# One-core vision layer with a state scan: from state 7 on, every second term made by VectorE in PSUM, the other states' decays in SBUF, scans in one piece

## The chip, the core and the metric

The kernel runs on one core of a Trainium2 chip. Its time is device microseconds from start to end of one execution. The kernel before took 352.08 us, the median of three runs (351.4 to 352.4). One further execution was recorded by the profiler: 354.25 us in all, of which the instructions span 351.9 us. All times below are microseconds unless marked ns.

In the rows, POOL is GpSimd, DVE is VectorE, ACT is ScalarE, PE is TensorE's matmul, PEld its weight load and SP the queue that issues the transfers.

## The reference, cut to what matters

Four images of 1024 tokens with 64 features go through three blocks: token mixing by retention, a selective state scan, and a two-layer feed-forward with routed experts, with a layer norm behind the second and the third. The scan is what the change touches. Per image, with 128 inner channels and 16 states:

```python
x_conv = silu(x_main @ W_conv + b_conv)
B_proj, C_proj = split(x_conv @ W_bc + b_bc)          # 16 states each
dt = softplus(x_conv @ W_dt + b_dt)
def scan_step(h, inputs):                             # over the 1024 tokens
    A_bar = exp(dt_t[..., None] * A)                  # decay
    B_bar = dt_t[..., None] * B_t[:, None, :]
    h_new = A_bar * h + B_bar * x_t[..., None]        # decay * h + term
    y_t = (h_new * C_t[:, None, :]).sum(axis=-1)
```

The kernel takes u = dt * x once per image. For each state s it needs the decay exp(dt * A[:, s]), the term u * B[s], the scan h, and the product hc = h * C[s]; the 16 products are then summed.

## The kernel before

Channels lie on the 128 partitions and tokens on the free dimension, so one state of one image is a job on 128x1024 float32. A `Job` has an image, a state, a first token, a number of halves (of 512 tokens) and `at`, its place counted in halves. Images 0 to 2 have 16 jobs of two halves each. Image 3 is in `SPLIT`: it has 32 jobs of one half, and the change leaves their work as it is.

Each job passes over four engines:

- ScalarE makes the decay (`decay_exp`). It goes either to `slot`, one pair of PSUM banks (the profile calls it `decay`), or to `decay_own` in SBUF.
- The term is made in one of two ways. For a job in `GPSIMD_JOBS`, GpSimd multiplies u by the row of B into the SBUF ring `ub` (`drive` on GpSimd), and the decay is in `slot`. For a job in `VECTOR_JOBS`, ScalarE copies u into `slot` (`fill_slot`), VectorE multiplies it there by the row of B (`drive` on VectorE, the rows `decay<-decay,b_row`), and the decay is in `decay_own`.
- VectorE scans (`scan_job`): h = factor * h + term. In either way one of the two inputs lies in PSUM and the other in SBUF.
- GpSimd makes hc = h * C (`weigh`), and TensorE adds hc up in PSUM (`states_out`).

In images 0 to 2 before, the vector jobs are states 0, 4, 8, 10 and 14. GpSimd has 11 terms and 16 products per image.

There is only one `slot`, so each job's fill waits for the scan of the job before. From state 7 on (`halved`) the scan and the fill go by halves of 512 tokens: ScalarE fills one bank while VectorE scans the other, and the second half's scan starts from the last column of the first.

The order on every engine is written out by hand in steps: phase p is image p's scan, and step n is its state n; k numbers the steps. In step k VectorE scans job k. GpSimd does `weigh` for job k-1 and then `drive` for job k+1, so the order of its queue is: product of k-1, term of k+1, product of k, term of k+2, and so on, with no term where the job is a vector job. ScalarE fills the slot for job k+1 near the start of step k and makes the `decay_own` of job k+2 at its end. VectorE's queue in the same steps also carries the head of the next image (`weight_scores` in steps 0 to 7, `prelu` in 8, `step_sizes` in 12, `inputs` in 13, which makes the next u) and the tail of the image before (`last_part`). The b and c rows come by transfers from SP three and two steps ahead.

In this document "product k" is the POOL instruction hc of state k, "term k" is the POOL instruction ub of state k, and "the late part" of an image is what runs from its state 7 to state 0 of the next image.

Of the kernel before, what the change touches and what calls it, by code (L numbers as in the profile page):

```python
# [46 lines left out]
for _b in range(IMAGES):  # L47
    for _first in (0, HALF) if _b in SPLIT else (0,):
        for _s in range(STATES):
# [7 lines left out]
               if job.state in ((0, 4, 8, 10, 14) if job.image not in SPLIT else range(0, STATES, 2))]  # L57
# [70 lines left out]
def vit_layer(nc, xT, gammaT, packed, routed_w, route, out):  # L128
    with ExitStack() as ctx:
        def sb(name, shape, dt=F32):  # L130
            return ctx.enter_context(nc.sbuf_tensor(name, shape, dt))
# [39 lines left out]
        ub = sb("ub", [P, 3 * T])  # L171
        decay_own = sb("decay_own", [P, T])
# [133 lines left out]
        def end_of(q):  # L306
            return JOBS[q].at + JOBS[q].halves
# [31 lines left out]
        def halved(q):  # L339

            return JOBS[q].halves == 2 and JOBS[q].state >= TILES - 1
# [5 lines left out]
        def ring(at, halves):  # L347

            return slice(at % 6 * HALF, (at % 6 + halves) * HALF)

# [547 lines left out]
        def _(act):  # L898
# [20 lines left out]
            def own_decay(q):  # L919

                made, halves = vector_made(q), JOBS[q].halves
                if made >= 2:

                    act.wait_ge(scan_done, end_of(job_with(vector_made, VECTOR_JOBS, made + halves - 3)))
                decay_exp(q, decay_own[:, two_banks(made, halves)], tokens(q))

            def fill_slot(q):

                job = JOBS[q]
                if on_vector(q) and job.state == 0 and job.first == 0:  # L930
                    act.wait_ge(u_ready, job.image + 1)
                if q == 0:
                    act.wait_ge(next_read, 3)
                in_halves = job.halves == 2 and q > 0 and halved(q - 1)
                for at, halves in ((job.at, 1), (job.at + 1, 1)) if in_halves else ((job.at, job.halves),):
                    if at + halves > 2:

                        act.wait_ge(scan_done, at + halves - 2)
                    first = job.first + (at - job.at) * HALF
                    columns = slice(first, first + halves * HALF)  # L940
                    if on_vector(q):
                        nc.scalar.activation(slot[:, two_banks(at, halves)], u[:, job.image % 2, columns], ACT.Copy)\  # L942
                            .then_inc(u_copied, halves)
                    else:
                        decay_exp(q, slot[:, two_banks(at, halves)], columns)
# [164 lines left out]
            for p in PHASES:  # L1110
                for n in range(STEPS):
# [3 lines left out]
                    for i, (start, end) in enumerate(parts(p, n)):  # L1115
                        for q in begun(start + 2, end + 2):
                            fill_slot(q)
# [23 lines left out]
                        for q in range(len(JOBS)):  # L1141
                            if own_limit(start) <= JOBS[q].at < own_limit(end) and on_vector(q):
                                own_decay(q)
# [19 lines left out]
        def _(pool):  # L1163
# [17 lines left out]
            def drive(q):  # L1181
# [6 lines left out]
                if made + job.halves > 6:  # L1188

                    pool.wait_ge(scan_done, end_of(job_with(gpsimd_made, GPSIMD_JOBS, made + job.halves - 7)))  # L1190
                nc.gpsimd.tensor_tensor(ub[:, ring(made, job.halves)], u[:, job.image % 2, tokens(q)],  # L1191
# [25 lines left out]
        def _(dve):  # L1217
# [88 lines left out]
            def scan_job(q):  # L1306

                job = JOBS[q]
                for at, halves in ((job.at, 1), (job.at + 1, 1)) if halved(q) else ((job.at, job.halves),):
                    done = at + halves - job.at  # L1310
                    here = two_banks(at, halves)
                    if on_vector(q):
                        drive(q, here, ring(at, halves), vector_made(q) + done)
                        factor, term = decay_own[:, two_banks(vector_made(q) + at - job.at, halves)], slot[:, here]
                    else:
                        dve.wait_ge(ub_ready, gpsimd_made(q) + job.halves)
                        factor, term = slot[:, here], ub[:, ring(gpsimd_made(q) + at - job.at, halves)]
                    dve.wait_ge(decay_ready, at + halves)
                    if at + halves > 6:
                        dve.wait_ge(hc_ready, at + halves - 6)  # L1320
                        old = JOBS[JOB_OF[at + halves - 7]]
                        if old.halves == 1 and old.first == 0:
                            dve.wait_ge(carry_saved, old.state + 1)
                    initial = 0.0
                    if at > job.at:
                        dve.wait_ge(scan_done, at)
                        initial = h[:, ring(at - 1, 1).stop - 1:ring(at - 1, 1).stop]
                    elif job.first:
                        dve.wait_ge(carry_saved, job.state + 1)
                        initial = carry[:, job.state:job.state + 1]  # L1330
                    nc.vector.tensor_tensor_scan(h[:, ring(at, halves)], factor, term, initial, ALU.mult, ALU.add)\  # L1331
                        .then_inc(scan_done, halves)
# [223 lines left out]
```

## Time and profile before

| | |
|---|---|
| median of three runs | 352.08 us |
| profiled execution, whole / its span | 354.25 / 351.9 us |
| POOL busy | 259.5 us (74%), 136 instructions |
| DVE busy | 262.4 us (75%), 287 instructions |
| ACT busy | 191.0 us (54%), 298 instructions |
| PE busy | 280.4 us (80%), 1426 instructions |
| mean granted TensorE clock | 0.902 |

Busy shares are averages over unlike stages. The scans of images 0 to 2 fill the span from about 45 to 255 us, and there the busy digits of DVE and POOL are 8 or 9 nearly throughout. Matmuls are pipelined, so PE's share is not a measure of its peak. A stretch is best read from where a given product starts to where a later one starts, since GpSimd does them in a fixed order.

### The profile page before, as it was taken

The numbers are of one execution on the slowest core, as the hardware profiler recorded it, in microseconds if no ns is written. First come the engines' busy times: TensorE is split into PE (matmuls) and PEld (weight loads), VectorE is DVE, ScalarE is ACT, GpSimd is POOL, SyncE is SP. The second block draws the span as 40 slices with busy tenths as digits, with TensorE's granted clock in tenths as the row PEclk, the third lists the DMA queues.
The fourth block names the chain that finished last, engine by engine and source line by source line (L and its number), as shares of the span: only waits on it lengthen the run. The fifth ranks groups of instructions, "written<-read, shape, count | busy, mean of one in ns | idle before, by whom it ended". The sixth has DMA issues, their size and how long they took to land.

```text
span 351.9 us, 4676 instructions
## 1 busy us (share of the span) xinstructions
PE 280.4 (80%) x1426; PEld 160.4 (46%) x1426; DVE 262.4 (75%) x287; ACT 191.0 (54%) x298; POOL 259.5 (74%) x136
## 2 busy tenths in 40 slices
PE   8998838784965889998895999977647846887996
PEld 5423402332453343465632434756434535636664
DVE  2466669989778989987989899879988766249420
ACT  2105823337895243689674337893785843357532
POOL 1027067998999999999999799899978889349300
PEclk9999959998789899999999899987976995588999
DMA  7960596766699997776999877678999999536200
GB/s 234 417 258 0 160 313 225 236 249 257 226 306 304 278 394 270 240 277 193 325 307 374 284 239 235 244 233 278 321 304 313 296 309 340 163 122 177 45 2 15
DMA packets 47128, 85.88 MB, mean 244 GB/s; under 512 B 7936, under 2 KB 24832, under 8 KB 46848
## 3 DMA queue, kind: packets, MB, share of 16 engines
q1 hardware_dynamic: 46704, 84.43, 72.8%
q10 hardware_dynamic: 400, 1.17, 1.1%
q8 instruction: 11, 0.18, 0.2%
q14 instruction: 13, 0.11, 0.1%
HBM read 75.62 MB, written 1.57 MB: 219 GB/s over the span
## 4 chain that ended last, share of the span: by engine, by line
PE 24%; DVE 13%; ACT 9%; DMA 6%; issue 4%; POOL 3%; SPq 2%; DVEq 0%; POOLq 0%; ACTq 0%
DVE h L1331 9%; PE acc_y L661 5%; PE tail L720 4%; DMA c_row<-bc_dram 4%; POOL ub L1191 2%; PE acc_r L614 2%; DMA b_row<-bc_dram 2%; PE work L603 2%; DVE decay L1303 2%; ACT decay L915 1%; PE work L752 1%; POOL hc L1202 1%; PE decay L537 1%; ACT decay_own L915 1%; ACT decay L942 1%
## 5 line engine op out<-in xcount | busy, mean ns | idle before, releaser
L1202 POOL TENSOR_TENSOR hc<-h,c_row 128x1024 f32<-128x1024 f32 (+1 forms) x79 | 154.3, 1961 | 30.0 <-DVE h L1331 24.4
L1191 POOL TENSOR_TENSOR ub<-u,b_row 128x1024 f32<-128x1024 f32 (+1 forms) x49 | 98.1, 2003 | 17.2 <-DVE u L1377 11.6
L661 PEld LDWEIGHTS acc_y<-pack,hc 128*128 128x128 f32 x512 | 63.8, 154 | 48.7 <-issue 34.7
L661 PE MATMUL acc_y<-pack,hc 128*128 128x128 f32 x512 | 78.2, 298 | 9.4 <-ACT y_t L1025 4.9
L915 ACT ACTIVATE decay<-delta,neg_a 128x512 f32<-128x512 f32 (+1 forms) x64 | 51.3, 812 | 62.7 <-DVE h L1331 62.1
L1331 DVE TENSOR_TENSOR_SCAN h<-decay,ub 128x512 f32<-128x512 f32 (+1 forms) x41 | 66.0, 1609 | 12.4 <-POOL ub L1191 6.4
L603 PE MATMUL work<-q,kT 64*128 64x512 f32 x112 | 33.7, 679 | 18.4 <-DVE mixed L1357 14.1
L942 ACT ACTIVATE decay<-u 128x512 f32<-128x512 f32 (+1 forms) x42 | 26.5, 640 | 30.4 <-DVE h L1331 30.2
L1303 DVE TENSOR_TENSOR decay<-decay,b_row 128x512 f32<-128x512 f32 (+1 forms) x40 | 30.8, 769 | 14.4 <-DMA b_row<-bc_dram 8.6
L1357 DVE TENSOR_TENSOR mixed<-gam,work 128x512 f32<-128x512 f32 x56 | 35.5, 676 | 7.9 <-PE work L603 7.1
L614 PE MATMUL acc_r<-mixed,v_sb 128*64 128x512 f32 x128 | 36.9, 657 | 1.1 <-DVE mixed L1357 1.0
L1331 DVE TENSOR_TENSOR_SCAN h<-decay_own,decay 128x512 f32<-128x512 f32 (+1 forms) x23 | 34.5, 1498 | 1.1
L915 ACT ACTIVATE decay_own<-delta,neg_a 128x512 f32<-128x512 f32 (+1 forms) x31 | 28.5, 918 | 1.5 <-DVE delta L1370 1.4
L720 PEld LDWEIGHTS tail<-f,group_w 128*128 128x128 f32 x192 | 27.6, 221 | 0.4
L720 PE MATMUL tail<-f,group_w 128*128 128x64 f32 x192 | 26.8, 301 | 0.0
L1331 DVE TENSOR_TENSOR_SCAN h<-decay,h,ub 128x512 f32<-128x512 f32 x18 | 23.1, 1283 | 2.5
L603 PEld LDWEIGHTS work<-q,kT 64*128 64x128 f32 x112 | 8.9, 193 | 34.2 <-DVE mixed L1357 23.9
L1176 POOL TENSOR_TENSOR expert_w<-expert_w 128x2048 f32<-128x2048 f32 x2 | 9.0, 4520 | 15.3 <-DMA expert_w<-routed_w 15.3
L614 PEld LDWEIGHTS acc_r<-mixed,v_sb 128*64 128x64 f32 x128 | 6.6, 141 | 26.6 <-issue 18.2
L715 PE MATMUL tail<-onehot,bias_w 96*128 96x512 bf16 x12 | 5.1, 426 | 14.2 <-ACT f L1055 7.1
L1331 DVE TENSOR_TENSOR_SCAN h<-decay_own,h,decay 128x512 f32<-128x512 f32 x9 | 11.5, 1280 | 0.3
L981 ACT ACTIVATE hT<-acc_r,pack 128x512 f32<-128x512 f32 x4 | 2.7, 675 | 15.8 <-PE acc_r L614 15.8
(206 smaller groups left out, 347.0 us busy)
## 6 DMA issues: line engine op xcount, KB each, us to landing
b_row<-bc_dram SPq DMA_DIRECT2D x64, 512.0 KB, 5.3
c_row<-bc_dram SPq DMA_DIRECT2D x64, 512.0 KB, 5.9
group_w<-expert_w SPq DMA_DIRECT2D x48, 128.0 KB, 5.0
gam<-gammaT SPq DMA_DIRECT2D x8, 512.0 KB, 10.6
expert_w<-routed_w SPq DMA_DIRECT2D x1, 2048.0 KB, 18.4
gam<-expert_w SPq DMA_DIRECT2D x16, 128.0 KB, 4.7
x_in<-xT SPq DMA_DIRECT2D x4, 256.0 KB, 9.0
pack<-packed ACTq DMA_DIRECT2D x1, 788.0 KB, 6.7
```

The costliest lines, as they stand in the source:

```text
L603: nc.tensor.matmul(pair[:, i * HALF:(i + 1) * HALF], kT[D * i:D * i + D, j * P:(j + 1) * P], q2[D * i:D * i + D, :], start=True, stop=True ...
L614: mm = nc.tensor.matmul(acc_r[D * i:D * i + D, :], v_sb[:, j, :], mixed[:, j % 2, i * HALF:(i + 1) * HALF], start=(j == 0), stop=(j == TIL ...
L661: mm = nc.tensor.matmul(acc_y[:, to:to + P], hc[:, at:at + P], ident, start=(job.state == 0 and c % 4 == 0), stop=(job.state == STATES - 1 ...
L720: mm = nc.tensor.matmul(bank[:, (g % 8) * GROUP:(g % 8 + 1) * GROUP], group_w[:, g, layer, :], f[:, g * GROUP:(g + 1) * GROUP], start=Fals ...
L915: op = nc.scalar.activation(target, delta[:, job.image % 2, columns], ACT.Exp, scale=neg_a[:, job.state:job.state + 1])
L942: nc.scalar.activation(slot[:, two_banks(at, halves)], u[:, job.image % 2, columns], ACT.Copy)\
L1176: nc.gpsimd.tensor_tensor(w, w, expert_w[:, layer, EXPERTS, :].unsqueeze(1) .broadcast_to([P, EXPERTS, HID]), ALU.add).then_inc(s_cw, 1)
L1191: nc.gpsimd.tensor_tensor(ub[:, ring(made, job.halves)], u[:, job.image % 2, tokens(q)], b_row[:, ring(job.at, job.halves)], ALU.mult).the ...
L1202: nc.gpsimd.tensor_tensor(hc[:, here], h[:, here], c_row[:, here], ALU.mult).then_inc(hc_ready, job.halves)
L1303: nc.vector.tensor_tensor(slot[:, here], slot[:, here], b_row[:, columns], ALU.mult).then_inc(ub_own, halves)
L1331: nc.vector.tensor_tensor_scan(h[:, ring(at, halves)], factor, term, initial, ALU.mult, ALU.add)\
L1357: nc.vector.tensor_tensor(mixed[:, j % 2, at], gam[:, j, at], pair[:, at], ALU.mult).then_inc(read, 1)
```

## The change

In images 0 to 2:

- State 12 becomes a vector job too, so that from state 8 on all even states are, and GpSimd has 10 terms per image instead of 11.
- `KEPT_JOBS` are the jobs whose decay is kept in SBUF: all vector jobs and, new, the GpSimd jobs 7, 9, 11, 13 and 15. Those five have their decay in `decay_own` and their term in `ub`, and do not use `slot` at all. `SLOT_JOBS` are the jobs that do use it.
- `decay_own` has room for two whole jobs instead of one (a ring of four halves, `two_rows`), and `ub` for two instead of three.
- The slot's fill waits for the last job that used the same bank (`slot_left`), not for the job before.
- `halved` goes: from state 7 on scans, multiplies, fills and copies cover all 1024 tokens in one instruction.

```diff
 VECTOR_JOBS = [q for q, job in enumerate(JOBS)
-               if job.state in ((0, 4, 8, 10, 14) if job.image not in SPLIT else range(0, STATES, 2))]
+               if job.state in ((0, 4, 8, 10, 12, 14) if job.image not in SPLIT else range(0, STATES, 2))]
+KEPT_JOBS = [q for q, job in enumerate(JOBS)
+             if q in VECTOR_JOBS or job.image not in SPLIT and job.state in (7, 9, 11, 13, 15)]
+SLOT_JOBS = [q for q in range(len(JOBS)) if q in VECTOR_JOBS or q not in KEPT_JOBS]
...
-        ub = sb("ub", [P, 3 * T])
-        decay_own = sb("decay_own", [P, T])
+        ub = sb("ub", [P, 2 * T])
+        decay_own = sb("decay_own", [P, 2 * T])
...
+        def kept_made(q):
+
+            return sum(JOBS[s].halves for s in KEPT_JOBS if s < q)
+
+        def slot_left(q):
+
+            used = [s for s in SLOT_JOBS if s < q and (JOBS[q].halves == 2 or JOBS[s].halves == 2
+                                                       or JOBS[s].at % 2 == JOBS[q].at % 2)]
+            return end_of(used[-1]) if used else 0
...
+        def two_rows(made, halves):
+
+            return slice(made % 4 * HALF, (made % 4 + halves) * HALF)
...
             def own_decay(q):
 
-                made, halves = vector_made(q), JOBS[q].halves
-                if made >= 2:
-
-                    act.wait_ge(scan_done, end_of(job_with(vector_made, VECTOR_JOBS, made + halves - 3)))
-                decay_exp(q, decay_own[:, two_banks(made, halves)], tokens(q))
+                made, halves = kept_made(q), JOBS[q].halves
+                if made + halves > 4:
+
+                    act.wait_ge(scan_done, end_of(job_with(kept_made, KEPT_JOBS, made + halves - 5)))
+                decay_exp(q, decay_own[:, two_rows(made, halves)], tokens(q))
...
-                in_halves = job.halves == 2 and q > 0 and halved(q - 1)
-                for at, halves in ((job.at, 1), (job.at + 1, 1)) if in_halves else ((job.at, job.halves),):
-                    if at + halves > 2:
-
-                        act.wait_ge(scan_done, at + halves - 2)
...
+                if slot_left(q):
+                    act.wait_ge(scan_done, slot_left(q))
+                if on_vector(q):
+                    nc.scalar.activation(slot[:, two_banks(job.at, job.halves)], u[:, job.image % 2, tokens(q)], ACT.Copy)\
+                        .then_inc(u_copied, job.halves)
+                else:
+                    decay_exp(q, slot[:, two_banks(job.at, job.halves)], tokens(q))
...
             def scan_job(q):
 
                 job = JOBS[q]
...
+                here, end = two_banks(job.at, job.halves), end_of(q)
+                if on_vector(q):
+                    drive(q, here, ring(job.at, job.halves), vector_made(q) + job.halves)
+                    term = slot[:, here]
+                else:
+                    dve.wait_ge(ub_ready, gpsimd_made(q) + job.halves)
+                    term = ub[:, two_rows(gpsimd_made(q), job.halves)]
+                dve.wait_ge(decay_ready, end)
+                factor = decay_own[:, two_rows(kept_made(q), job.halves)] if q in KEPT_JOBS else slot[:, here]
...
+                nc.vector.tensor_tensor_scan(h[:, ring(job.at, job.halves)], factor, term, initial, ALU.mult, ALU.add)\
+                    .then_inc(scan_done, job.halves)
```

On VectorE's queue in image 0, from state 7 to state 10 (a scan is listed there as SCALAR_TENSOR_TENSOR with h on the left), before:

```order
L1331 SCALAR_TENSOR_TENSOR h<-decay,ub 128x512
L1331 SCALAR_TENSOR_TENSOR h<-decay,h,ub 128x512
L1303 TENSOR_TENSOR decay<-decay,b_row 128x512
L1331 SCALAR_TENSOR_TENSOR h<-decay_own,decay 128x512
L1303 TENSOR_TENSOR decay<-decay,b_row 128x512
L1331 SCALAR_TENSOR_TENSOR h<-decay_own,h,decay 128x512
L1362 SCALAR_TENSOR_TENSOR hT<-acc_r,neg_ba,hT 128x512
L1331 SCALAR_TENSOR_TENSOR h<-decay,ub 128x512
L1331 SCALAR_TENSOR_TENSOR h<-decay,h,ub 128x512
```

and after:

```order
L1336 SCALAR_TENSOR_TENSOR h<-decay_own,ub 128x1024
L1312 TENSOR_TENSOR decay<-decay,b_row 128x1024
L1336 SCALAR_TENSOR_TENSOR h<-decay_own,decay 128x1024
L1367 SCALAR_TENSOR_TENSOR hT<-acc_r,neg_ba,hT 128x512
L1336 SCALAR_TENSOR_TENSOR h<-decay_own,ub 128x1024
L1312 TENSOR_TENSOR decay<-decay,b_row 128x1024
L1336 SCALAR_TENSOR_TENSOR h<-decay_own,decay 128x1024
```

The scans of states 7 and 9 read both inputs from SBUF (`decay_own` and `ub`), a form that VectorE's queue before does not hold; those of 8 and 10 keep one input in PSUM.

On GpSimd's queue in image 0, from product 9 to product 13 (term k is ub, product k is hc), before:

```order
L1202 TENSOR_TENSOR hc<-h,c_row 128x1024
L1191 TENSOR_TENSOR ub<-u,b_row 128x1024
L1202 TENSOR_TENSOR hc<-h,c_row 128x1024
L1191 TENSOR_TENSOR ub<-u,b_row 128x1024
L1202 TENSOR_TENSOR hc<-h,c_row 128x1024
L1191 TENSOR_TENSOR ub<-u,b_row 128x1024
L1202 TENSOR_TENSOR hc<-h,c_row 128x1024 x2
```

and after:

```order
L1211 TENSOR_TENSOR hc<-h,c_row 128x1024
L1200 TENSOR_TENSOR ub<-u,b_row 128x1024
L1211 TENSOR_TENSOR hc<-h,c_row 128x1024 x2
L1200 TENSOR_TENSOR ub<-u,b_row 128x1024
L1211 TENSOR_TENSOR hc<-h,c_row 128x1024 x2
```

Before, this reads product 9, term 11, product 10, term 12, product 11, term 13, products 12 and 13. After, term 12 is gone: product 9, term 11, products 10 and 11, term 13, products 12 and 13.

## Rows read from the trace of the kernel before

**Rows 1.** The page's busy times: us, share of the span, instructions.

```profile
PE 280.4 (80%) x1426; PEld 160.4 (46%) x1426; DVE 262.4 (75%) x287; ACT 191.0 (54%) x298; POOL 259.5 (74%) x136
```

**Rows 2.** Busy time by stretch: from product 7 to the next image's product 0 (three rows), then from product 0 to product 7 (images 1, 2).

```profile
core 0: us, PE busy (x) PEld busy (x) DVE busy (x) ACT busy (x) POOL busy (x), PEclk, DMA share, GB/s
80.60:118.22 37.62, 25.84 (x121) 14.64 (x120) 31.33 (x31) 26.51 (x40) 35.73 (x15) 0.83 0.82 276
148.16:186.42 38.26, 33.00 (x206) 21.07 (x204) 33.79 (x35) 29.37 (x45) 35.78 (x16) 1.00 0.84 274
217.62:255.28 37.66, 30.12 (x182) 21.66 (x182) 33.08 (x35) 28.51 (x45) 35.84 (x17) 0.91 0.82 267
118.22:148.16 29.94, 27.59 (x135) 12.32 (x133) 27.50 (x27) 14.47 (x17) 28.00 (x12) 0.99 0.90 299
186.42:217.62 31.20, 27.80 (x131) 11.90 (x132) 28.14 (x27) 14.85 (x17) 27.93 (x12) 0.95 0.83 283
```

**Rows 3.** POOL in order of time, image 1's products 6, 7: start, us, instruction, [idle before].

```profile
145.32 2.36 POOL L1202 TENSOR_TENSOR hc<-h,c_row 128x1024 f32<-128x1024 f32 x1
148.16 2.35 POOL L1202 TENSOR_TENSOR hc<-h,c_row 128x1024 f32<-128x1024 f32 x1 [0.49 <-DVE h L1331]
150.47 2.36 POOL L1191 TENSOR_TENSOR ub<-u,b_row 128x1024 f32<-128x1024 f32 x1
152.78 2.36 POOL L1202 TENSOR_TENSOR hc<-h,c_row 128x1024 f32<-128x1024 f32 x1
```

**Rows 4.** Who waited for whom, 148.16 to 186.42: total us, times, longest.

```profile
POOL hc L1202 <- DVE h L1331: 3.0, 5, 0.9
...
DVE h L1331 <- POOL ub L1191: 1.2, 2, 1.0
...
DVE decay L1303 <- ACT decay L942: 0.8, 1, 0.8
```

**Rows 5.** Groups of the whole span by form: busy us, mean ns, idle before.

```profile
L1331 DVE TENSOR_TENSOR_SCAN h<-decay_own,decay 128x1024 f32<-128x1024 f32 x6 | 13.7, 2286 | 0.5
...
L1331 DVE TENSOR_TENSOR_SCAN h<-decay,h,ub 128x512 f32<-128x512 f32 x18 | 23.1, 1283 | 2.5
L1331 DVE TENSOR_TENSOR_SCAN h<-decay_own,decay 128x512 f32<-128x512 f32 x17 | 20.7, 1220 | 0.6
...
L1303 DVE TENSOR_TENSOR decay<-decay,b_row 128x1024 f32<-128x1024 f32 x6 | 7.4, 1229 | 1.2 <-issue 1.1
```

**Rows 6.** Groups by form on ACT: exponentials and copies, half and whole.

```profile
L915 ACT ACTIVATE decay<-delta,neg_a 128x512 f32<-128x512 f32 x46 | 31.2, 691 | 14.9 <-DVE h L1331 14.5
...
L915 ACT ACTIVATE decay_own<-delta,neg_a 128x1024 f32<-128x1024 f32 x15 | 17.1, 1137 | 1.4 <-DVE delta L1370 1.4
...
L942 ACT ACTIVATE decay<-u 128x512 f32<-128x512 f32 x38 | 22.4, 599 | 22.4 <-DVE h L1331 22.4
...
L942 ACT ACTIVATE decay<-u 128x1024 f32<-128x1024 f32 x4 | 4.1, 1028 | 8.0 <-DVE h L1331 7.8 <-DVE u L1377 0.2
```

**Rows 7.** DVE where u is made in images 0, 1 and 2.

```profile
105.00 1.20 DVE L1377 TENSOR_TENSOR u<-delta,mixed 128x1024 f32<-128x1024 f32 x1
...
172.57 1.20 DVE L1377 TENSOR_TENSOR u<-delta,mixed 128x1024 f32<-128x1024 f32 x1
...
242.49 1.20 DVE L1377 TENSOR_TENSOR u<-delta,mixed 128x1024 f32<-128x1024 f32 x1
```

**Rows 8.** POOL at the same three places, product 13.

```profile
105.22 3.20 POOL L1202 TENSOR_TENSOR hc<-h,c_row 128x1024 f32<-128x1024 f32 x1 [0.49 <-DVE h L1331]
...
172.79 3.20 POOL L1202 TENSOR_TENSOR hc<-h,c_row 128x1024 f32<-128x1024 f32 x1 [0.50 <-DVE h L1331]
...
242.71 3.19 POOL L1202 TENSOR_TENSOR hc<-h,c_row 128x1024 f32<-128x1024 f32 x1 [0.50 <-DVE h L1331]
```

**Rows 9.** ACT's copy of u for state 10, and DVE's last scan of state 13, image 1.

```profile
156.05 1.12 ACT L942 ACTIVATE decay<-u 128x512 f32<-128x512 f32 x2
...
171.38 1.28 DVE L1331 TENSOR_TENSOR_SCAN h<-decay,h,ub 128x512 f32<-128x512 f32 x1
```

**Rows 10.** DVE in image 1: the scan of state 8's second half, then prelu.

```profile
150.50 1.28 DVE L1331 TENSOR_TENSOR_SCAN h<-decay_own,h,decay 128x512 f32<-128x512 f32 x1
151.69 0.73 DVE L1362 SCALAR_TENSOR_TENSOR hT<-acc_r,neg_ba,hT 128x512 f32<-128x512 f32 x1
```

More of the change, by code:

```diff
@@ L337, in job_with @@
             return [q for q in jobs if made(q) <= piece < made(q) + JOBS[q].halves][0]
-        def halved(q):
-            return JOBS[q].halves == 2 and JOBS[q].state >= TILES - 1
+        def kept_made(q):
[4 more added lines that the diff above has]
+            return end_of(used[-1]) if used else 0
         def ub_made(q):
@@ L933, in fill_slot @@
                     act.wait_ge(next_read, 3)
-                in_halves = job.halves == 2 and q > 0 and halved(q - 1)
-                for at, halves in ((job.at, 1), (job.at + 1, 1)) if in_halves else ((job.at, job.halves),):
-                    if at + halves > 2:
-                        act.wait_ge(scan_done, at + halves - 2)
[L939 to L945, printed above, removed]
+                if slot_left(q):
[5 more added lines that the diff above has]
+                    decay_exp(q, slot[:, two_banks(job.at, job.halves)], tokens(q))
             def save_carry(q):
@@ L1141, in _ @@
                         for q in range(len(JOBS)):
-                            if own_limit(start) <= JOBS[q].at < own_limit(end) and on_vector(q):
+                            if own_limit(start) <= JOBS[q].at < own_limit(end) and q in KEPT_JOBS:
                                 own_decay(q)
@@ L1187, in drive @@
                 pool.wait_ge(b_loaded[k % 3], 16 * (k // 3 + 1))
-                if made + job.halves > 6:
-                    pool.wait_ge(scan_done, end_of(job_with(gpsimd_made, GPSIMD_JOBS, made + job.halves - 7)))
-                nc.gpsimd.tensor_tensor(ub[:, ring(made, job.halves)], u[:, job.image % 2, tokens(q)],
+                if made + job.halves > 4:
+                    pool.wait_ge(scan_done, end_of(job_with(gpsimd_made, GPSIMD_JOBS, made + job.halves - 5)))
+                nc.gpsimd.tensor_tensor(ub[:, two_rows(made, job.halves)], u[:, job.image % 2, tokens(q)],
                                         b_row[:, ring(job.at, job.halves)], ALU.mult).then_inc(ub_ready, job.halves)
@@ L1308, in scan_job @@
                 job = JOBS[q]
[L1309 to L1332, printed above, removed]
@@ new lines, in scan_job @@
+                if end > 6:
+                    dve.wait_ge(hc_ready, end - 6)
+                    old = JOBS[JOB_OF[end - 7]]
+                    if old.halves == 1 and old.first == 0:
+                        dve.wait_ge(carry_saved, old.state + 1)
+                initial = 0.0
+                if job.first:
+                    dve.wait_ge(carry_saved, job.state + 1)
+                    initial = carry[:, job.state:job.state + 1]
+                nc.vector.tensor_tensor_scan(h[:, ring(job.at, job.halves)], factor, term, initial, ALU.mult, ALU.add)\
+                    .then_inc(scan_done, job.halves)
```

3 lines of the change are left out of this document (2 added, 1 removed).

## The prediction

> **What bounds the kernel now.** I read the busy times first, then the stretches of the scans, then GpSimd's queue in order of time, then the waits. The page shows DVE and POOL nearly equal, 262.4 and 259.5 us of 351.9 [rows 1]: neither can be called the bound from that. The stretches tell more. In the late part of each image (product 7 to the next image's product 0, 37.62, 38.26 and 37.66 us, mean 37.85) POOL is busy 35.7 to 35.8 us and DVE 31.3 to 33.8 [rows 2]. In the early part DVE and POOL are both near 28 of 30 to 31 us. So in the late part, the only one that the change rewrites, GpSimd is the fullest engine: 9 products and 6 terms of 2.36 us, one behind the other at a spacing of 2.31 (150.47 to 152.78) [rows 3]. What is left of the 38.26 us is 3.0 us in which a product waited for its scan, in 5 pieces [rows 4]. DVE waits for terms 1.2 us and for the copy of u 0.8 us there, so the single slot costs DVE little; it is POOL's queue that sets the pace.
>
> **What the change takes off.** By form, the two halves of a scan take 1.22 + 1.28 = 2.50 us and one whole scan 2.29 [rows 5]: 0.21 less for each of 27 scans (9 late states, 3 images), 5.7 us of DVE. The multiply in PSUM takes 1.23 us whole [rows 5]; the three new ones (state 12) cost DVE 3.7 us. DVE so gains about 2 us over three images, on an engine that has 4 to 6 us of slack per late part [rows 2]: worth nothing by itself. On POOL three terms go, 3 x 2.31 = 6.9 us, and these are on the path. ACT pays 1.14 us for a kept decay in place of 2 x 0.69, and 1.03 for a copy in place of 2 x 0.60 [rows 6]; state 12 adds it a copy, 0.8 us net. ACT is busy 29.4 of 38.3 us [rows 2], so either sign is hidden, except for one place, below. The exponential for job k+2 now waits for scan k and stands at the end of ScalarE's step k; behind it in its queue are the copy for job k+2 and the tail's pieces of step k+1. Before, the second half of each fill waited for the same scan k and stood earlier in the step, so nothing on ACT gets later by it. The ub ring of two costs nothing: GpSimd's term k+1 is issued behind product k-1, whose scan is at or behind the last reader of the buffer it reuses.
>
> **What it adds: scans with both inputs in SBUF.** 15 scans (states 7, 9, 11, 13, 15 of three images) now read `decay_own` and `ub`. No scan before does. The nearest rows are the three u = delta * x, the DVE instructions with two SBUF inputs that run beside GpSimd. At 105.00, 172.57 and 242.49 u takes its usual 1.20 us [rows 7], and POOL's product 13, which starts 0.22 us later, takes 3.20, 3.20 and 3.19 [rows 8] instead of 2.36 [rows 3]. That is 0.84 us more, of the 0.98 that it lies beside u. Products beside other DVE work (scans and multiplies with an operand in PSUM) all keep 2.35 to 2.38. So GpSimd stands nearly still while VectorE reads two operands from SBUF.
>
> The bounds for one such scan: nothing (2.29 us on DVE, POOL undisturbed; I see no reason for a gain), up to 2.29 us of POOL at a standstill plus a whole POOL instruction, 2.36, for which DVE waits first. I take a standstill of the whole scan, by the u rows, and work out from the queue's order what of DVE's wait counts.
>
> The Trainium skill, "SBUF — State Buffer", section "Who interferes with whom", says that a VectorE instruction with two SBUF inputs contends with a GpSimd instruction that reads SBUF, and that the shared port pair is held by one of them for the whole instruction, whoever was first. The trace agrees for the case in which VectorE was first (0.84 us); GpSimd first is not shown by any row before. By this rule the sum would be the one below; its opposite is a rival.
>
> **The walk of one pair of states**, t = 0 where term 9 is done. GpSimd goes on with product 8 at once (scan 8 is done by then), so scan 9 and product 8 want SBUF together. In whichever order, one after the other: 2.31 + 2.29 us. Product 9 waits for scan 9, hands over in 0.13 us (scan 13 ends at 171.38 + 1.28 = 172.66 [rows 9], product 13 starts at 172.79 [rows 8]), and is followed by term 11. VectorE's multiply and scan of state 10 (1.23 + 2.29) fall beside those two undisturbed, since one of their operands is in PSUM. The pair costs POOL three instructions and a standstill, 3 x 2.31 + 2.29 + 0.17 (0.13 and 0.04 for the way to DVE) = 9.4 us. DVE needs 5.8 us for the pair, up to 2.3 of waiting, and at most 1.95 of other work in the steps 11 and 12: 10.1 us, but scan 13 then meets product 12 still running, so POOL's count holds.
>
> **The sum.** Product 7 to the next product 0: 14 POOL instructions x 2.31 = 32.3; four standstills (scans 9, 11, 13, 15) x 2.46 = 9.8; and the 0.84 beside u as before. Together 43.0 against 37.85: +5.1 us. The standstill of scan 7 lies before product 7: product 6 to product 7 takes 2.31 + 2.46 = 4.8 us instead of 2.84 (145.32 to 148.16) [rows 3]: +1.9. Per image +7.0 to +7.2, in three images +21 to +22. The other check: 5 x 2.46 = 12.3 added, one term (2.3) and the idle of 2.8 absorbed, 7.2. The early parts (29.94 and 31.20 us) have about 2 to 3 us of idle on POOL [rows 2], but the product order couples them to scans of their own, so I give nothing back. On the profiled execution, 354.25 + 21.7 = 376; on the median, which is 2.2 lower, 352.1 + 21.7 = 373.8. I forecast 374.
>
> **The one place on ACT.** Scan 8 ends at 150.50 + 1.28 = 151.8 [rows 10], and the copy of u for state 10 starts at 156.05, behind the table load and the convolution [rows 9]. With 1.03 for a whole copy, the multiply of state 10 can start 5.3 us after scan 8's end. In the walk scan 9 ends about 5.9 us after scan 8's end, so this is just hidden. If scan 9 isn't held up, that cover is gone, which enters the first rival.
>
> **Rivals.**
>
> *A. No contention (faster).* The scan doesn't keep GpSimd from SBUF, because it is not a plain multiply. For it: the scan takes 2.29 us for 1024 columns where a multiply takes 1.23 [rows 5], so it asks for data half as often. Against it: the u rows. Then the pair costs POOL 3 x 2.31 + 0.14 = 7.1 us. Late part: 32.3 + 0.84 + 0.14 x 4, plus about 1.4 us where DVE is late by step sizes and two tail pieces before scan 13, and 0.7 from the copy of state 10: 35.8 to 36.5, which is 1.4 to 2.0 less than 37.85. Three images: -4 to -6, 347 us. This decides if the standstill per scan is below about 0.4 us.
>
> *B. Each element read costs GpSimd a cycle, no lock.* For 1024 elements POOL loses what it lost beside u, 0.84 to 0.98 us, once per scan, and goes on in between; DVE never waits. For it: the u rows fit just as well, since a multiply asks for data all the time. Against A's 35.8 to 36.5: four times 0.9 less some 0.9 that falls in DVE's late pieces, +2.7, and +0.9 before product 7. Late part about 38.9, product 6 to 7 unchanged to +0.5: +1.1 to +1.5 per image, +4: 356 us.
>
> *C. More than the walk.* Waits on both sides don't overlap: each of the 15 scans also delays a later one by the 2.36 us of DVE's wait. That bounds it above: 374 + 15 x 2.36 = 409. The walk excludes most of it, since DVE has 3.6 us of slack per pair (9.4 against 5.8).
>
> That the change doesn't do what it says isn't open: the queues of the changed kernel show the form `h<-decay_own,ub`.
>
> **Chances and range.** The standstill (likeliest) 0.68, own range 366 to 384: the low end if the early parts give back 2 to 3 us per image, the high end if DVE's wait counts four or five times. A 0.17, B 0.11, C (above 384) 0.04. The range of 8 in 10: 347 to 383, which leaves out C and half of A. A difference of 0.3% is 1.1 us, about what a measurement of this kernel can tell from no change. Faster by more than that: A and a sliver of B, 0.18. Within: 0.04. Slower: 0.78.
>
> **What would show it.** The scans `h<-decay_own,ub` read longer than 2.29 us, up to 4.6 (GpSimd first), or POOL's products beside them read up to 4.6 us instead of 2.36 (DVE first). The late part goes from 37.85 to about 43 us, product 6 to 7 from 2.84 to 4.8; POOL instructions per late part go from 15 to 14; the early parts stay at 30 to 31, and image 3 is unchanged. DVE's scans with a PSUM operand stay at 2.29. The forecast is wrong if the new scans read 2.29 and POOL keeps 2.36 beside them (A), or if POOL's products read about 3.2 (B).

## The result, and the profile after

The changed kernel takes 368.57 us, the median of four runs (368.1 to 370.3; a fifth took 366.8), beside 352.24 us for the kernel before (four runs). The ratio is 1.046, with a 95% interval of 1.041 to 1.051: slower by 16 us. The profiled execution took 370.3 us, its span 368.2. The forecast was 374 us and a standstill of GpSimd beside the new scans. A few executions, of the kernel before and of one other, ran some per cent slower as a whole; every ratio, and the times of the last run of experiment 7, leave them out.

The page's busy line of the changed kernel:

```profile
PE 296.0 (80%) x1426; PEld 173.6 (47%) x1426; DVE 287.4 (78%) x254; ACT 189.6 (51%) x275; POOL 254.5 (69%) x133
```

DVE has 33 instructions fewer than in [rows 1] and is busy 25.0 us longer. The groups by form say where that is. The first of these DVE groups is the new form (columns as in [rows 5]):

```profile
L1336 DVE TENSOR_TENSOR_SCAN h<-decay_own,ub 128x1024 f32<-128x1024 f32 x15 | 63.0, 4201 | 8.5 <-POOL ub L1200 6.0 <-issue 2.1 <-ACT decay_own L928 0.3
L1336 DVE TENSOR_TENSOR_SCAN h<-decay_own,decay 128x1024 f32<-128x1024 f32 x18 | 41.2, 2286 | 1.6
```

The scan with one input in PSUM reads 2.29 us as before. The same scan with both inputs in SBUF reads 4.20 in the mean. GpSimd in order of time, image 0, from product 6 on:

```profile
77.65 2.36 POOL L1211 TENSOR_TENSOR hc<-h,c_row 128x1024 f32<-128x1024 f32 x1
82.29 2.35 POOL L1211 TENSOR_TENSOR hc<-h,c_row 128x1024 f32<-128x1024 f32 x1 [2.28 <-DVE h L1336]
84.60 2.36 POOL L1200 TENSOR_TENSOR ub<-u,b_row 128x1024 f32<-128x1024 f32 x1
86.91 2.35 POOL L1211 TENSOR_TENSOR hc<-h,c_row 128x1024 f32<-128x1024 f32 x1
91.54 2.36 POOL L1211 TENSOR_TENSOR hc<-h,c_row 128x1024 f32<-128x1024 f32 x1 [2.28 <-DVE h L1336]
```

and VectorE beside the first of them:

```profile
77.79 4.37 DVE L1336 TENSOR_TENSOR_SCAN h<-decay_own,ub 128x1024 f32<-128x1024 f32 x1 [0.97 <-issue]
82.08 1.20 DVE L1312 TENSOR_TENSOR decay<-decay,b_row 128x1024 f32<-128x1024 f32 x1
```

Product 6 starts at 77.65 and ends at 80.01. Scan 7 starts 0.14 us after it, at 77.79, and ends at 82.16: it makes its 2.15 us of progress once product 6 is over. Only then can product 7 go. This repeats at every second state, so a pair of states takes 9.25 us from product to product (82.29 to 91.54), and 9.25 to 9.28 wherever the prediction's walk applies, against its 9.4. The stretches that answer to [rows 2] (late part of images 0, 1, 2, then image 1's early part with product 6 to 7):

```profile
82.29:124.87 42.58, 27.04 (x112) 14.74 (x112) 38.56 (x21) 24.49 (x30) 33.42 (x14) 0.73 0.79 252
155.95:198.65 42.70, 35.47 (x196) 23.59 (x196) 40.05 (x25) 26.80 (x34) 33.50 (x14) 0.88 0.80 252
231.31:273.66 42.35, 31.12 (x170) 23.46 (x171) 39.47 (x26) 26.50 (x36) 35.51 (x16) 0.82 0.79 257
124.87:155.95 31.08, 29.34 (x147) 13.26 (x145) 29.11 (x26) 16.54 (x20) 27.98 (x13) 0.99 0.81 278
```

| stretch | before | after | difference | forecast |
|---|---|---|---|---|
| three late parts | 113.54 | 127.63 | +14.1 | +15.3 |
| product 6 to 7, three times | 8.55 | 13.96 | +5.4 | +5.7 |
| product 0 to 6, three times | 83.77 | 82.77 | -1.0 | 0 |
| image 3, from its first product to the end | 96.62 | 94.54 | -2.1 | 0 |

The prediction's terms per image, 5.1 and 1.9, make 21.0 in this table; it went on with 21.7, from its other check. With the first product 0.12 us earlier, this is the whole 16.3 us between the spans.

The last late part shows the other order, in which a GpSimd instruction finds VectorE's scan before it. At the seam to image 3 GpSimd has a half-size term behind product 14, while scan 15 (started at 264.71, 4.38 us) is waiting:

```profile
264.59 2.35 POOL L1211 TENSOR_TENSOR hc<-h,c_row 128x1024 f32<-128x1024 f32 x1
266.90 3.25 POOL L1200 TENSOR_TENSOR ub<-u,b_row 128x512 f32<-128x512 f32 x1
```

That term takes 1.27 us elsewhere. Here scan 15 gets its turn when product 14 ends, and the term loses 1.98 us to it. This is far more than the 0.84 to 0.98 that rival B allowed for the reads of one scan.

### The profile page after: what moved, and what is told of

Same layout as the page of the kernel before. It is cut to its first block and busy times, and to the rows that moved or that the text cites. A ratio compares the mean times of both kernels' runs of the same rounds, so it can differ in the third digit from the quotient of the medians.

```text
span 368.2 us, 4607 instructions
## 1 busy us (share of the span) xinstructions
PE 296.0 (80%) x1426; PEld 173.6 (47%) x1426; DVE 287.4 (78%) x254; ACT 189.6 (51%) x275; POOL 254.5 (69%) x133
## 5 line engine op out<-in xcount | busy, mean ns | idle before, releaser
L674 PE MATMUL acc_y<-pack,hc 128*128 128x128 f32 x512 | 83.3, 311 | 15.3 <-POOL hc L1211 11.6
L1336 DVE TENSOR_TENSOR_SCAN h<-decay_own,ub 128x1024 f32<-128x1024 f32 x15 | 63.0, 4201 | 8.5 <-POOL ub L1200 6.0
L928 ACT ACTIVATE decay_own<-delta,neg_a 128x1024 f32<-128x1024 f32 (+1 forms) x49 | 49.1, 1004 | 22.6 <-DVE h L1336 18.0
L928 ACT ACTIVATE decay<-delta,neg_a 128x512 f32<-128x512 f32 (+1 forms) x31 | 27.8, 897 | 51.2 <-DVE h L1336 51.0
L1336 DVE TENSOR_TENSOR_SCAN h<-decay_own,decay 128x1024 f32<-128x1024 f32 (+1 forms) x26 | 50.9, 1958 | 1.9
L1336 DVE TENSOR_TENSOR_SCAN h<-decay,ub 128x1024 f32<-128x1024 f32 (+1 forms) x23 | 44.0, 1911 | 3.4 <-ACT decay L928 2.7
L1312 DVE TENSOR_TENSOR decay<-decay,b_row 128x1024 f32<-128x1024 f32 (+1 forms) x34 | 32.8, 966 | 8.0 <-DMA b_row<-bc_dram 4.6
L950 ACT ACTIVATE decay<-u 128x1024 f32<-128x1024 f32 (+1 forms) x34 | 28.0, 825 | 20.3 <-DVE h L1336 20.1
L733 PEld LDWEIGHTS tail<-f,group_w 128*128 128x128 f32 x192 | 35.9, 278 | 1.6 <-issue 0.7
L733 PE MATMUL tail<-f,group_w 128*128 128x64 f32 x192 | 34.6, 359 | 0.0
L1336 DVE TENSOR_TENSOR_SCAN h<-decay_own,carry,decay 128x512 f32<-128x512 f32 x8 | 10.2, 1280 | 0.3
```

The source lines that it names most:

```text
L674: mm = nc.tensor.matmul(acc_y[:, to:to + P], hc[:, at:at + P], ident, start=(job.state == 0 and c % 4 == 0), stop=(job.state == STATES - 1 ...
L733: mm = nc.tensor.matmul(bank[:, (g % 8) * GROUP:(g % 8 + 1) * GROUP], group_w[:, g, layer, :], f[:, g * GROUP:(g + 1) * GROUP], start=Fals ...
L928: op = nc.scalar.activation(target, delta[:, job.image % 2, columns], ACT.Exp, scale=neg_a[:, job.state:job.state + 1])
L950: nc.scalar.activation(slot[:, two_banks(job.at, job.halves)], u[:, job.image % 2, tokens(q)], ACT.Copy)\
L1312: nc.vector.tensor_tensor(slot[:, here], slot[:, here], b_row[:, columns], ALU.mult).then_inc(ub_own, halves)
L1336: nc.vector.tensor_tensor_scan(h[:, ring(job.at, job.halves)], factor, term, initial, ALU.mult, ALU.add)\
```

## The experiments

All are changes of one of the two kernels; their times stand beside runs of the kernel before on the same chip (352.1 to 353.6 us in the median), and a ratio is to those.

### 1. The decays go to the slot again

```diff
 KEPT_JOBS = [q for q, job in enumerate(JOBS)
-             if q in VECTOR_JOBS or job.image not in SPLIT and job.state in (7, 9, 11, 13, 15)]
+             if q in VECTOR_JOBS]
```

> The changed kernel, but the decays of states 7, 9, 11, 13 and 15 go into the PSUM slot again (scans in one piece, state 12 by VectorE, two-deep ub stay). Theory (a scan with both inputs in SBUF and a GpSimd instruction cannot run side by side): the late scans read 2.29 us again instead of 4.36, GpSimd's 2.28 us of idle before every second product goes, and what remains is ScalarE's fill in series with a whole scan, about 1.1 us per late state where VectorE has no other work: 350 to 358 us. Rival (the loss comes from the whole scans, from state 12 on VectorE or from the shallower ub): the time stays at 365 to 372 us.

Measured: 365.47 us (363.7 to 368.9), ratio 1.035 (1.029 to 1.041). The trace did what the theory said of the holds: all scans of 1024 tokens read 2.28 to 2.29 us. But the time is far above the expected 350 to 358 and lies in the rival's range, 365 to 372. These are its DVE groups and its three late parts:

```profile
L1336 DVE TENSOR_TENSOR_SCAN h<-decay,ub 128x1024 f32<-128x1024 f32 x30 | 68.7, 2289 | 14.6 <-ACT decay L928 13.3 <-POOL ub L1200 1.3
...
L1312 DVE TENSOR_TENSOR decay<-decay,b_row 128x1024 f32<-128x1024 f32 x18 | 22.1, 1230 | 16.5 <-ACT decay L950 11.2 <-issue 5.2
```

```profile
80.10:121.14 41.04, 29.44 (x124) 17.44 (x124) 31.00 (x21) 26.67 (x33) 33.55 (x14) 0.72 0.80 262
150.31:195.12 44.81, 39.28 (x206) 26.37 (x205) 33.40 (x25) 29.65 (x38) 33.64 (x14) 0.85 0.83 261
225.98:267.33 41.35, 31.54 (x176) 23.30 (x175) 31.23 (x24) 28.44 (x37) 33.72 (x16) 0.83 0.77 253
```

In the whole span these groups wait 24.5 us for ScalarE's fills (13.3 + 11.2). In the three late parts alone VectorE waits 22.3 us for fills, where the kernel before has 6.8. So a loss of 12 us stands without a single hold. It isn't the whole scans' alone: state 12 on VectorE is in it too, and by itself it costs 8 us (experiment 2), so whole scans and the shallower `ub` add about 4. Image 1 is 3.5 us longer than the others and has the granted clock at 0.50 from 172 to 180 (see experiment 4). The changed kernel pays for holds, this one for fills.

### 2. State 12 by VectorE, alone in the kernel before

```diff
-               if job.state in ((0, 4, 8, 10, 14) if job.image not in SPLIT else range(0, STATES, 2))]
+               if job.state in ((0, 4, 8, 10, 12, 14) if job.image not in SPLIT else range(0, STATES, 2))]
```

> The kernel before with one part of the change alone: state 12's term by VectorE in PSUM, all else as before (halves, one slot, ub of three). Theory (GpSimd's queue sets the pace of the late part): one term of 2.31 us less per image, of which VectorE's two multiplies of 0.69 us take back a part: late part 36.0 to 37.3 us instead of 37.85, total 346 to 351 us. Rival (VectorE and GpSimd bound it together): 351 to 355 us, no gain or a small loss.

Measured: 361.28 us (359.7 to 363.9), ratio 1.023 (1.019 to 1.028). Both theories are wrong: it is 8 us slower. GpSimd has one instruction less per late part, and the late parts are longer:

```profile
80.30:119.68 39.38, 28.17 (x122) 17.06 (x121) 32.53 (x33) 27.45 (x41) 33.53 (x14) 0.75 0.85 268
149.34:191.38 42.04, 35.72 (x206) 23.77 (x204) 35.14 (x37) 30.21 (x46) 33.59 (x14) 0.92 0.82 265
222.62:262.11 39.49, 31.60 (x181) 23.38 (x182) 33.91 (x36) 29.29 (x45) 33.65 (x15) 0.83 0.82 262
```

Product 11 to product 12 goes from 4.63 us to 6.01. ScalarE there, in image 1 (start, us, instruction):

```profile
162.75 0.45 ACT L967 ACTIVATE mixed<-acc_r,pack 128x256 f32<-128x256 f32 x1
...
164.81 0.67 ACT L1014 ACTIVATE work<-work,pack 128x512 f32<-128x512 f32 x1
165.38 1.17 ACT L915 ACTIVATE decay_own<-delta,neg_a 128x1024 f32<-128x1024 f32 x1
166.42 1.14 ACT L942 ACTIVATE decay<-u 128x512 f32<-128x512 f32 x2
```

and VectorE:

```profile
164.84 0.67 DVE L1392 TENSOR_SCALAR f<-tail 128x512 f32<-128x512 f32 x1
167.07 0.70 DVE L1303 TENSOR_TENSOR decay<-decay,b_row 128x512 f32<-128x512 f32 x1 [1.56 <-ACT decay L942]
```

At the same place in the kernel before, scan 12 starts with

```profile
165.37 1.22 DVE L1331 TENSOR_TENSOR_SCAN h<-decay,ub 128x512 f32<-128x512 f32 x1 [1.04 <-POOL ub L1191]
```

ScalarE is busy without a gap from the eviction of B and C through the softplus pieces, the exponential and the copy. VectorE's multiply waits 1.56 us for that copy (1.56 in image 2 too, 2.15 in image 0). The two multiplies and this wait come to 2.9 us in VectorE's chain, where before a wait of 1.04 us for GpSimd's term stood: +1.8 us, the difference of the late parts of images 0 and 2. In image 1 the clock comes on top (experiment 4). The chain scan 11, scan 12, scan 13 was as near the bound as GpSimd's queue, and products cannot run ahead of scans.

### 3. A shorter copy

```diff
+                        cut = 64 if job.state == 12 and job.halves == 2 else halves * HALF
```

> State 12 alone on VectorE, and ScalarE copies only 64 of every 512 tokens of u for state 12 (the rest of that state's term is left out, so this measures the wait, not a whole kernel). Theory (ScalarE's queue of softplus pieces, exponential and copy makes VectorE's multiply of state 12 late by 1.6 us, so the cover that the prediction gave ScalarE's work isn't there): VectorE's wait before that multiply falls from 1.56 us to 0.4 to 1.2, and product 11 to product 12 from 6.01 us to 5.0 to 5.6. Rival (VectorE's own work makes it long): product 11 to 12 stays above 5.8.

Measured (one run of 356.66 us, which has no interval): the wait falls only to 1.19 us in images 1 and 2, and product 11 to 12 from 6.01 to 5.63 there. In image 0 the wait hardly falls (2.15 to 2.11), and product 11 to 12 stays at 5.97. That is at or just beyond the weak end of what the theory expected, and below the rival's 5.8 in two images of three. The copy itself is a small part; what stands ahead of it in ScalarE's queue is the larger one, as the rows above suggest. How the rest divides is not settled.

### 4. TensorE's clock in image 1

In experiment 2 the late part of image 1 is 2.6 us longer than the other two. The granted clock stands at 0.50 (the 1.2 GHz level) there. In the 4 us before it fell TensorE was busy 1.7 us, where in the same 4 us of the kernel before it was busy 3.0 and the clock stayed at 1.00:

```profile
168.00:170.00 2.00, 0.57 (x6) 0.33 (x4) 1.97 (x3) 1.97 (x3) 1.75 (x1) 1.00 0.81 311
170.00:172.00 2.00, 1.13 (x2) 0.30 (x2) 2.00 (x3) 1.72 (x4) 0.93 (x1) 1.00 0.71 156
172.00:178.00 6.00, 4.99 (x24) 4.91 (x25) 5.38 (x7) 2.41 (x4) 3.78 (x2) 0.50 1.03 307
```

The edit on top of experiment 2 repeats products with the same result:

```diff
-                    mm = queries(acc_r)
+                    for _ in range(3):
+                        mm = queries(acc_r)
...
-                    mm = keys(use == SIDE_K1, acc_r[:, :])
+                    for _ in range(4 if use == SIDE_K0 else 1):
+                        mm = keys(use == SIDE_K1, acc_r[:, :])
```

> State 12 alone on VectorE (as in the run before), and TensorE does the queries' products of step 11 three times and the first keys' product of step 12 four times over, with the same results, to keep it busy there. Theory (the late part of image 1 is 2.6 us longer than that of images 0 and 2, 42.0 against 39.4, because the granted clock stands at 0.5 from 172 to 178 us): the clock stays at 1.0 there, the late part of image 1 falls to 39.3 to 40.5 us and the time by 1 to 3 us, to 358 to 360. Rival (the clock costs nothing, ScalarE or the transfers make it long): the late part of image 1 keeps 41.5 us or more. The late parts of images 0 and 2 change by less than 1 us in either case.

```profile
150.59:190.52 39.93, 36.99 (x220) 22.84 (x218) 35.06 (x37) 30.12 (x46) 33.58 (x14) 1.00 0.84 259
```

The clock stays at 1.00, and the late part of image 1 falls from 42.04 to 39.93 us, level with the others (39.82 and 39.31). VectorE's one wait for TensorE's `work` in that late part, near its end, falls from 1.92 to 0.48 us. So the slower step brought a slower clock with it, and the clock cost about 2.1 us. The total is 360.40 us (358.8 to 360.5), ratio 1.025 (1.019 to 1.031): against 1.023 (1.019 to 1.028) this doesn't resolve as a gain.

The same edit on the changed kernel:

> The changed kernel with the same repeated products. Theory (its late parts are set by GpSimd's instructions and the scans with two SBUF inputs one after the other, so TensorE's clock is hidden): late part of image 1 from 42.70 to 42.5 to 42.8 us, time within 1.5 us of 368.6, whatever the clock does. Rival (the clock has a part in the loss of the changed kernel): it falls by 2 us or more.

Measured: 371.01 us (370.7 to 371.7), ratio 1.055 (1.049 to 1.061), so 2.4 us slower. Both the time (within 1.5 us was expected) and the late part of image 1 (44.00 us, 42.5 to 42.8 expected) were misses. Nor did the edit hold the clock at 1.00. Here is the low stretch of the changed kernel, then that of this run:

```profile
173.00:181.60 8.60, 6.61 (x27) 5.82 (x28) 8.36 (x8) 3.32 (x4) 6.99 (x3) 0.52 0.79 234
...
174.40:181.20 6.80, 5.78 (x26) 5.67 (x27) 6.56 (x8) 2.36 (x3) 6.29 (x3) 0.50 0.70 244
```

So this run can't tell what the clock costs. Images 0 and 2 keep their late parts (42.57 and 42.33); in image 1, 1.3 us come between product 13 and 14 (6.85 in place of 5.57), where product 14 waits 1.34 us for TensorE: the repeated products got in the way there. The changed kernel's own trace tells more. Its three pairs of states from product 7 to 13 of image 1 take the same time, whatever the clock:

```profile
155.95:165.22 9.27, 8.42 (x58) 6.23 (x58) 9.02 (x6) 6.53 (x8) 6.99 (x3) 1.00 0.61 221
165.22:174.49 9.27, 4.52 (x26) 1.89 (x24) 7.78 (x4) 9.21 (x12) 6.99 (x4) 0.94 0.62 202
174.49:183.76 9.27, 8.77 (x35) 7.37 (x36) 9.03 (x8) 3.26 (x5) 6.99 (x4) 0.51 0.78 241
```

What it costs behind product 13 isn't shown apart; that late part is 0.1 us longer than image 0's.

### 5. What the 4.37 us of a scan are

The products that GpSimd does beside the new scans, cut to 64 tokens:

```diff
+                if job.halves == 2 and job.state in (6, 8, 10, 12, 14):
+                    here = slice(here.start, here.start + 64)
```

> The changed kernel with products 6, 8, 10, 12 and 14 of images 0 to 2 cut to the first 64 of 1024 tokens (their rest is left out, so this measures the scans, not a whole kernel). Theory (the 4.36 us of a scan with both inputs in SBUF are 2.1 us of waiting for the product that GpSimd started just before): these scans read 2.2 to 2.5 us, and GpSimd still idles about 2.3 us before the next product. Rival (the form itself is slow, with two SBUF inputs): they keep 4.2 to 4.4 us.

```profile
L1338 DVE TENSOR_TENSOR_SCAN h<-decay_own,ub x15: 2269/2292/2341, 77.5 to 255.3; 128x1024 f32<-128x1024 f32 x15
```

All 15 (min, median, max in ns) read the 2.29 us of any whole scan. The form is not slow; its time went into waiting for the product. GpSimd still idles 2.28 us and more before the next product. The run took 359.36 us (one run, without an interval), in spite of five products per image being cut to a sixteenth: late parts of 38.3, 43.8 and 39.3 us, as VectorE again waits for ScalarE (2.23 us before the multiply of state 10 in image 0).

The same products in two instructions:

```diff
+                    for i in range(2):
+                        part = slice(here.start + i * HALF, here.start + (i + 1) * HALF)
+                        nc.gpsimd.tensor_tensor(hc[:, part], h[:, part], c_row[:, part], ALU.mult).then_inc(hc_ready, 1)
```

> The changed kernel with products 6, 8, 10, 12 and 14 of images 0 to 2 as two GpSimd instructions of 512 tokens. Theory (SBUF is held for one instruction, and VectorE gets its turn between two of GpSimd's): the scans with both inputs in SBUF read 3.2 to 3.4 us instead of 4.36 (1.1 left of the first half, 2.15 of its own), the second half of the product reads 3.2 to 3.4 instead of 1.27, GpSimd's idle before the next product goes from 2.28 to under 0.3, and the time is within 1.5 us of 368.6, since the two still run one after the other. Rival (VectorE waits until GpSimd's queue has a gap): the scans keep 4.4 us and more. Rival (no hold, each element read costs a cycle): the second half reads at most 1.27 + 1.07 us and the time falls below 364.

```profile
159.21 3.28 DVE L1341 TENSOR_TENSOR_SCAN h<-decay_own,ub 128x1024 f32<-128x1024 f32 x1 [0.90 <-POOL ub L1200]
```

```profile
159.08 4.48 POOL L1214 TENSOR_TENSOR hc<-h,c_row 128x512 f32<-128x512 f32 x2
163.52 2.36 POOL L1216 TENSOR_TENSOR hc<-h,c_row 128x1024 f32<-128x1024 f32 x1
```

The two halves take 4.48 us instead of about 2.5 (two of 1.27) and end one behind the other with the scan between them. The scan reads 3.28 us: the rest of the first half and its own; the second half reads 3.25. So the hold lasts one instruction, and whoever waits comes next. The time, 366.62 us (366.1 to 368.7), ratio 1.038 (1.033 to 1.043), is 2 us below the changed kernel, a little more than the 1.5 expected: product 6 to product 7, which holds one standstill, takes 4.44 instead of 4.65 us.

### 6. One hold more, and one term more

State 12 by GpSimd with its decay in SBUF too:

```diff
-               if job.state in ((0, 4, 8, 10, 12, 14) if job.image not in SPLIT else range(0, STATES, 2))]
+               if job.state in ((0, 4, 8, 10, 14) if job.image not in SPLIT else range(0, STATES, 2))]
...
-             if q in VECTOR_JOBS or job.image not in SPLIT and job.state in (7, 9, 11, 13, 15)]
+             if q in VECTOR_JOBS or job.image not in SPLIT and job.state in (7, 9, 11, 12, 13, 15)]
```

> The changed kernel with state 12 left to GpSimd (its decay in SBUF too, so states 11, 12 and 13 scan with both inputs in SBUF): six such scans per image instead of five, eleven terms instead of ten. Theory (GpSimd's instructions and these scans run one after the other): one more term of 2.31 and one more standstill of 2.28 us per image, +13 to +15 us on 368.6: 381 to 384 us. Rival (the scans of this form cost a fixed loss that other work hides): +0 to +7, up to 376.

Measured: 379.17 us (378.5 to 380.6), ratio 1.073 (1.065 to 1.080). That is 2 us below the expected 381 to 384 and above the rival's 376. The late parts are 46.53, 46.56 and 46.28 us, +3.9 each, where +4.6 was expected. Scans 11 and 12 now hold up a term that stands directly behind a product:

```profile
98.24 4.33 POOL L1200 TENSOR_TENSOR ub<-u,b_row 128x1024 f32<-128x1024 f32 x1
```

Such a term loses 1.98 us, where GpSimd otherwise loses 2.32 from product to product (4.63 less 2.31). One term of 2.31 and one standstill of 1.98 more, and 0.34 less for scan 11's, make 3.95. Image 3 gave back 2.9 us.

State 12 by GpSimd with its decay in the slot, the five other holds kept (the first of the two edits alone):

> The changed kernel without its state-12 part: state 12's term by GpSimd again, its decay in the PSUM slot, the five scans with two SBUF inputs stay. Theory (with these scans, GpSimd's instructions and the scans in one line set the late part): one term of 2.31 us more per image, late part 42.5 to 44.9, +6 to +8 us on 368.6, so 374.5 to 377; the same part that made the kernel before 8 us slower is worth 7 us here. Rival (state 12 on VectorE costs here too, through ScalarE's queue, as it did alone): 360 to 368 us.

```profile
96.01 4.37 DVE L1336 TENSOR_TENSOR_SCAN h<-decay_own,ub 128x1024 f32<-128x1024 f32 x1 [1.40 <-POOL ub L1200]
102.62 2.29 DVE L1336 TENSOR_TENSOR_SCAN h<-decay,ub 128x1024 f32<-128x1024 f32 x1 [2.24 <-POOL ub L1200]
```

```profile
95.87 2.36 POOL L1211 TENSOR_TENSOR hc<-h,c_row 128x1024 f32<-128x1024 f32 x1
98.19 4.34 POOL L1200 TENSOR_TENSOR ub<-u,b_row 128x1024 f32<-128x1024 f32 x1
```

Measured: 372.18 us (371.6 to 374.4), ratio 1.062 (1.052 to 1.071), below the expected 374.5 to 377 and clearly above the rival's 368. The late parts are 44.55, 44.59 and 44.27, +1.9 each: a term of 2.31, less the 0.34 by which scan 11 costs GpSimd less when a term stands behind the product. Product 10 at 95.87 holds up scan 11; scan 11 then holds up term 12 (4.34 us instead of 2.36): the two are strictly in one line. Image 3 gave back 4.4 us against the changed kernel (90.19 and 94.54). The same move of state 12, which costs the kernel before 8 us, saves 3.6 us here.

### 7. Two tries for a faster kernel

Whole scans only where VectorE has other work behind, on top of experiment 2:

```diff
-            return JOBS[q].halves == 2 and JOBS[q].state >= TILES - 1
+            return JOBS[q].halves == 2 and JOBS[q].state >= TILES - 1 and JOBS[q].state not in (8, 12, 13)
```

> The kernel before with state 12's term by VectorE, and with the scans of states 8, 12 and 13 in one piece, where VectorE has other work behind the scan (prelu, step sizes, u) that covers ScalarE's fill of the slot. Theory: VectorE saves 0.21 us per whole scan and 0.13 per whole multiply, about 1 us per image, which counts where VectorE is now the later one: 0 to 3 us below the kernel with state 12 alone, 345 to 350 us. Rival (the fill is not covered): 1 to 3 us above it.

Measured: 364.64 us (362.4 to 367.3), ratio 1.031 (1.026 to 1.036). The theory failed: it is 3.4 us above experiment 2, just past the rival's 3. Late parts of 40.5, 45.9 and 40.4 us. VectorE waits 13.5 us for ScalarE's fills in them, where in experiment 2 it waits 11.9. In image 1 the granted clock is at 0.50 from 172 to 184, so the 45.9 is not the fills' alone.

The loads of the last image's weights two steps later, in the kernel before:

```diff
-                    if p == ALONE and n < TILES:
-                        for g in (2 * n, 2 * n + 1):
+                    if p == ALONE and 2 <= n < TILES + 2:
+                        for g in (2 * n - 4, 2 * n - 3):
```

> The kernel before, with the 16 loads of the last image's expert weights issued in steps 2 to 9 of image 3 instead of 0 to 7. Theory (image 3 is shorter after the change, 94.5 against 96.6 us, because SP's queue had caught up by then and the b rows came in time): moving other transfers off the first steps gives a part of this without the change: the waits for b rows (8.6 us on VectorE, 4.1 on GpSimd in the profile of before) fall and the time goes down by 0.5 to 2 us, to 350.5 to 352. Rival (the rows are late for want of transfer bandwidth, not of turns in SP's queue): within 0.5 us of the kernel before, or slower.

Measured: 350.80 us (348.4 to 353.3), ratio 0.998 (0.993 to 1.002). In the profile image 3 takes 93.9 us instead of 96.62, and VectorE's waits for b rows fall from 8.6 to 4.8 us, but the time does not resolve from that of the kernel before. No kernel of this study is shown to be faster.

## Why the prediction was right, and where it was wrong

- **GpSimd stands still beside a scan with two SBUF inputs: right**, and shown in both orders. The walk of a pair gave 9.4 us; the trace has 9.27. By the Trainium skill ("SBUF — State Buffer", "Who interferes with whom") the pair of ports is held for the whole instruction by whoever was first. The traces agree: 1.98 us lost by a term behind scan 15, 4.34 us for term 12 in experiment 6, and 2.1 us of waiting in scan 7, which goes when the product is short (experiment 5).
- **Its size: 0.14 us too large** per scan. I took 2.29 + 0.17 = 2.46; from product to product it adds 4.63 - 2.31 = 2.32, since a scan that waited ends 2.15 us after the product, and not 2.29. Over 15 scans this is 2.1 us, of the 5.4 by which 21.7 exceeded the 16.3 of the spans.
- **Nothing given back: wrong** by 3.1 us. The early parts gave 1.0, image 3 gave 2.1. In image 3 VectorE waits 4.6 us for b rows instead of 8.6. Experiment 7 shows that the order of SP's loads moves image 3 by 2.7 us in the profile. Why it is 90.2 us in one kernel and 97.5 in another stays open.
- **"It is POOL's queue that sets the pace": only half right**, and this is the step of the reasoning that failed, though the forecast's range held. [rows 4] showed 3.0 us of products waiting for scans, and I read them as slack. They were the sign of a second chain of the same length, from scan to scan over VectorE and ScalarE. Experiment 2 takes an instruction off GpSimd in each image and loses 8 us: in its profile 1.8 us per late part in that chain, and 2.1 by the clock.
- **"Either sign is hidden" on ScalarE: true of the changed kernel, but for a reason not checked.** In its three late parts VectorE waits for ScalarE 0.3 us in all, because the held scans make it late anyway. Without that cover it is wrong: in experiment 2 ScalarE has no gap in image 1 from 158.9 until well behind the copy at 166.4, and the copy for state 12 comes 1.56 us late. Its 29.4 busy us of 38.3 are an average. I had checked the copy for state 10 and not this one, which the change adds.
- **Rival A at 347 us: wrong also where there is no hold.** Its own case, decays in SBUF and no contention, can't be run. Two stand-ins without holds take 365 us (experiment 1, where fills wait instead) and 359 (short products, one run). As far as they tell, the kernel would be slower even without a hold, so the sign of the forecast didn't hang on it, and the holds cost 3 to 9 us on top, not 21.7. The sum that put all of the loss on the holds came near in part by luck: with the holds in place GpSimd's line is the longer one in images 0 and 2 (42.6 and 42.4 us against 38.3 to 41.4 in experiments 1 and 5) and covers ScalarE's lateness, which I had left out. In image 1, where all three have the lower clock for a time, those two take 44.8 and 43.8 us and the changed kernel 42.7.
- **ub of two, POOL with 14 instructions instead of 15, PSUM scans at 2.29: right** as read.

## What to carry to other kernels

Count GpSimd instructions and VectorE instructions with two SBUF inputs as one queue, and walk it in the order of issue: that gave a pair of states to within 0.2 us (9.4 and 9.27). Before calling a small wait slack, ask whether it is the place where a second chain of the same length ties in; here work moved off one of two such engines made the kernel slower. And check an engine's cover in the very step where its new instruction stands, not by its share of a stretch of 38 us.

## What the runs showed of the hardware that I had not expected

- A VectorE scan that waits for GpSimd's instruction is recorded as running: 4.37 us for one that needs 2.29 alone. It ends 2.15 us after the instruction it waited for, 0.14 us less than it takes alone.
- The turn changes between two GpSimd instructions that stand directly behind one another: a waiting scan gets in after the first (3.28 us with products in halves), and the second one waits, recorded as running too (3.25 us).
- TensorE's granted clock fell to 0.50 for 6 us in image 1 when the chain around it grew by 1.8 us, and that cost about 2.1 us of a late part (experiment 4). In the changed kernel a pair of states took 9.27 us at 0.51 as at 1.00.
